# LN1's weight and the q, k, v biases folded into the projection weights; one head of the split tile moved from GpSimd to VectorE

## What is computed

```python
def _ln(x, w, b):
    return (x - m) / jnp.sqrt(v + 1e-05) * w + b
xn = _ln(q_x, ln1_w, ln1_b)                 # q_x is already layer-normed once
q = (xn @ wq + bq); k = (xn @ wk + bk); v = (xn @ wv + bv)      # 16 heads of 16
fq, fk = elu(q) + 1, elu(k) + 1
# per token: mixing over its 16 heads, then a division
qkv = fq @ (fk^T v); qk = fq . sum over heads of fk
x = q_x + (qkv / (qk + 1e-6)) @ wo + bo
x = x + gelu(_ln(x) @ fc_w + fc_b) @ proj_w + proj_b
```

## Time and profile before

| | |
|---|---|
| median of 3 runs | 1744.97 us |
| profiled execution | 1744.85 us, of it a span of 1742.7 us |
| PE busy | 1680.7 us (96%), 7243 instructions |
| PE weight loads | 1227.5 us (70%) |
| VectorE | 1166.9 us (67%) |
| GpSimd | 1166.9 us (67%) |
| ScalarE | 904.1 us (52%) |

### The profile page before, as it was taken

The page is one execution under the profiler, slowest core; times in us unless marked ns, Lnnn a source line. Parts: engine busy times, 40 slices in busy tenths (PEclk is TensorE's granted clock), DMA queues, the critical chain, the costliest instruction groups (busy, mean ns, idle before and its releaser), DMA issues.

```text
span 1742.7 us, 25628 instructions
## 1 busy us (share of the span) xinstructions
PE 1680.7 (96%) x7243; PEld 1227.5 (70%) x7289; DVE 1166.9 (67%) x1968; ACT 904.1 (52%) x2240; POOL 1166.9 (67%) x624
## 2 busy tenths in 40 slices
PE   6899999999999999999999998989999999999997
PEld 4555666666666666666666665578888888888886
DVE  7989999999999999999999993322222222222221
ACT  4356667667667667667667646522322322332322
POOL 5769889889889889889889881413333343343343
PEclk9898999999999999999999999999999999999999
DMA  4302211211211211111111111367777777777764
GB/s 151 116 13 61 62 49 37 62 49 36 61 49 36 61 49 36 59 50 36 54 55 37 37 49 37 92 169 162 165 154 160 165 157 156 167 158 156 168 158 78
DMA packets 89455, 157.20 MB, mean 90 GB/s; under 512 B 8896, under 2 KB 72128, under 8 KB 89024
## 3 DMA queue, kind: packets, MB, share of 16 engines
q1 hardware_dynamic: 60512, 112.58, 20.9%
q0 software_dynamic: 28896, 44.06, 14.9%
HBM read 101.79 MB, written 48.56 MB: 86 GB/s over the span
## 4 chain that ended last, share of the span: by engine, by line
PE 89%; ACT 5%; DVE 2%; issue 2%; DMA 1%; POOL 1%; SPq 1%; POOLq 0%; ACTq 0%; DVEq 0%
PE p_b L1494 17%; PE p_b L1548 13%; PE p_b L1698 10%; PE p_b L1709 10%; PE p_b L1641 8%; PE p_q L1698 7%; PE p_q L1466 6%; PE p_v L1698 4%; PE p_v L1466 3%; PE p_b L1480 2%; PE p_xT L1685 2%; PE p_xT L1626 2%; ACT rows L706 1%; ACT xmid L706 1%; PE p_b L1588 1%
## 5 line engine op out<-in xcount | busy, mean ns | idle before, releaser
L654 POOL DMA_INDIRECT out_rows<-prod_pool,prod x142 | 221.4, 1559 | 387.9 <-ACT prod_pool L949 357.5
L523 POOL TENSOR_TENSOR prod_pool<-prod_pool 128x2048 f32<-128x2048 f32 (+1 forms) x180 | 347.9, 1933 | 14.1
L1548 PE MATMUL p_b<-bT,fc_sb 128*128 128x512 f32 x512 | 231.5, 606 | 1.3 <-ACT bT L865 1.3
L1494 PE MATMUL p_b<-proj_sb,hid 128*128 128x256 f32 x1024 | 230.5, 379 | 0.0
L1494 PEld LDWEIGHTS p_b<-proj_sb,hid 128*128 128x128 f32 x1024 | 189.6, 190 | 29.4 <-issue 0.5
L1026 DVE TENSOR_TENSOR prod<-p_q,eqk 128x4096 f32<-128x4096 f32 (+1 forms) x47 | 184.0, 3914 | 5.3 <-DVE attn L1076 1.0
L1698 PE MATMUL p_b<-prod,exp_up 128*128 128x256 f32 x840 | 187.1, 379 | 0.0
L1063 DVE TENSOR_REDUCE qkv<-prod 128x256 f32<-128x4096 f32 (+1 forms) x47 | 183.7, 3910 | 1.6
L1050 DVE TENSOR_TENSOR prod<-p_q,v_dve 128x2048 f32<-128x2048 f32 (+2 forms) x60 | 177.4, 2956 | 1.5
L574 POOL DMA_INDIRECT rows_sorted<-rows,slot x128 | 125.7, 982 | 78.5 <-issue 34.5
L1035 DVE TENSOR_REDUCE p_q<-prod 128x128 f32<-128x2048 f32 (+2 forms) x60 | 177.4, 2957 | 1.1
(11 more groups left out here) (208 smaller groups left out, 2988.6 us busy)
## 6 DMA issues: line engine op xcount, KB each, us to landing
exp_up<-in_experts SPq DMA_DIRECT2D x71, 768.0 KB
prod<-rows_sorted SPq DMA_DIRECT2D x71, 260.0 KB
xin<-in_x SPq DMA_DIRECT2D x16, 512.0 KB, 3.4
xres<-in_x SPq DMA_DIRECT2D x16, 512.0 KB
xres<-xmid POOLq DMA_DIRECT2D x16, 512.0 KB, 4.6
out_rows<-x SPq DMA_DIRECT2D x16, 512.0 KB, 2.9
exp_dn<-in_experts SPq DMA_DIRECT2D x8, 384.0 KB, 5.8
out_rows<-prod_pool,prod POOLq DMA_INDIRECT x142, 3.8
```

The source lines that it names most:

```text
L523: done(g.tensor_tensor(prod_pool[:, at:at + n * w], prod_pool[:, at:at + n * w], prod_pool[:, at + n * w:at + 2 * n * w], ALU.add))
L654: pool.indirect_dma_start(out=out[:, :], out_offset=bass.IndirectOffsetOnAxis(ap=tok_i[j][:, a:a + 1], axis=0), in_=yg[j][:, a * D:(a + 1) ...
L1494: ins = t_.matmul(o, src[:, k, t * P:(t + 1) * P], w[:, k, :], start=k == 0, stop=bias_at is None and k == chunks - 1)
L1548: ins = t_.matmul(bnk[:], fc_sb[:, k, f * P:(f + 1) * P], bT[:, k, :], start=k == 0, stop=k == KC - 1)
```

## The change

Three things. First, from tile n = 12 on (`FOLDED` = 3 blocks of 4) q, k and v are made from `wfold` instead of `wqkv_sb`: ACT scales the weights by LN1's weight once, PE makes the vector (ln1_b - ln1_w) @ W + bias by two small matmul groups, and VectorE adds a 256th of it to every row of the weights (the diff has two functions `fold()`, VectorE's first and then PE's). `take_x` then adds 1 to the normed x instead of applying weight and bias: the normed x of a token sums to zero over its width, so the ones bring in that vector whole. The bias matmuls are gone for those tiles, and `take_x` is one activation instead of two. Second, this folding is done once, at steps 0 and 1. Third, `POOL_HEADS` is 5, so VectorE has 11 heads of tile 2.

```diff
-POOL_HEADS = 6
+POOL_HEADS = 5
+FOLDED = 3
...
+        def folded(n):
+
+            return not isinstance(n, int) or n >= 4 * FOLDED
...
-                for k in range(KC):
-                    ins = a.activation(xnT[u % 2][:, k, :], p_xT[:, k * P:(k + 1) * P], ACT.Identity,
-                                       bias=ln_sb[:, 1, k:k + 1], scale=ln_sb[:, 0, k:k + 1])
+                if folded(n):
+                    ins = a.activation(xnT[u % 2][:].rearrange("p k t -> p (k t)"), p_xT[:, 0:D], ACT.Identity,
+                                       bias=one_1[:, 0:1])
...
+            def fold_parts():
+
+                for k in range(KC):
+                    a.activation(fold_d[:, k:k + 1], ln_sb[:, 0, k:k + 1], ACT.Identity, scale=-1.0,
+                                 bias=ln_sb[:, 1, k:k + 1]).then_inc(fold_diff, 1)
+                    a.activation(wfold[:, k, :], wqkv_sb[:, k, :], ACT.Copy, scale=ln_sb[:, 0, k:k + 1]
+                                 ).then_inc(fold_in, 1)
+                act.wait_ge(fold_diff, KC)
+                for k in range(KC):
+                    a.activation(fold_w[:, k, :], ident[:], ACT.Identity, scale=0.0, bias=fold_d[:, k:k + 1]
+                                 ).then_inc(fold_in, 1)
...
+                if first:
+                    fold_parts()
                 if more:
                     take_qkv(c + 1, 1)
...
+            def fold():
+
+                dve.wait_ge(fold_psum, 1)
+                dve.wait_ge(fold_in, 2 * KC)
+                for k in range(KC):
+                    for bnk, lo, hi in ((p_b0, 0, 512), (p_b1, 512, 768)):
+                        ins = v.scalar_tensor_tensor(wfold[:, k, lo:hi], bnk[:, 0:hi - lo], 1.0 / D, wfold[:, k, lo:hi],
+                                                     ALU.mult, ALU.add)
...
                     products_2(c, 1, False)
+                if isinstance(c, int) and c == 1:
+                    fold()
...
+                    w = wfold if folded(n) else wqkv_sb
...
-                    if isinstance(n, int) and n == 0:
-                        pe.wait_ge(bias_ready, 1)
-                    for bnk, lo, hi in parts:
-                        ins = t_.matmul(bnk[:, 0:hi - lo], bias_rows_bf[:], bias_bf[:, lo:hi],
-                                        start=False, stop=True)
+                    if not folded(n):
...
+            def fold():
+
+                pe.wait_ge(fold_in, 2 * KC)
+                wait(pe, attnT_ready, KC)
+                for bnk, lo, hi in ((p_b0, 0, 512), (p_b1, 512, 768)):
+                    for k in range(KC):
+                        t_.matmul(bnk[:, 0:hi - lo], fold_w[:, k, :], wqkv_sb[:, k, lo:hi], start=k == 0, stop=False)
+                    ins = t_.matmul(bnk[:, 0:hi - lo], bias_rows_bf[:], bias_bf[:, lo:hi], start=False, stop=True)
...
                     project_x(c, 2, "P")
+                if isinstance(c, int) and c == 1:
+                    fold()
```

More of the change, by code:

```diff
@@ L84, in build @@
         wqkv_sb = sb("wqkv_sb", [P, KC, 3 * D])
+        wfold = sb("wfold", [P, KC, 3 * D])
+        one_1 = sb("one_1", [P, 1])
+        fold_d = sb("fold_d", [P, KC])
         wo_sb = sb("wo_sb", [P, KC, D])
@@ L200, in build @@
         first_s2 = first_s2.rearrange("p (h g) -> p h g", h=HEADS)
+        fold_w = sg_u[:, 1, 0:KC * P].rearrange("p (k n) -> p k n", k=KC)
         first_v = sg_u[:, 0, 0:D].rearrange("p (e g) -> p e g", e=HD)
@@ L257, in build @@
         qkv_taken = sem("qkv_taken")
+        fold_diff = sem("fold_diff")
+        fold_in = sem("fold_in")
+        fold_psum = sem("fold_psum")
+        fold_ready = sem("fold_ready")
         feat_ready = sem("feat_ready")
@@ L674, in take_x @@
                 wait(act, qkv_psum, n - 1)
-                for k in range(KC):
-                    ins = a.activation(xnT[u % 2][:, k, :], p_xT[:, k * P:(k + 1) * P], ACT.Identity,
-                                       bias=ln_sb[:, 1, k:k + 1], scale=ln_sb[:, 0, k:k + 1])
+                if folded(n):
+                    ins = a.activation(xnT[u % 2][:].rearrange("p k t -> p (k t)"), p_xT[:, 0:D], ACT.Identity,
+                                       bias=one_1[:, 0:1])
+                else:
+                    for k in range(KC):
+                        ins = a.activation(xnT[u % 2][:, k, :], p_xT[:, k * P:(k + 1) * P], ACT.Identity,
+                                           bias=ln_sb[:, 1, k:k + 1], scale=ln_sb[:, 0, k:k + 1])
                 ins.then_inc(xnT_ready, 1)
@@ L1136, in first_block @@
                 dve.sem_inc(pq_free, 1)
+            def fold():
[5 more added lines that the diff above has]
+                                                     ALU.mult, ALU.add)
+                        if k < KC - 1 or lo == 0:
+                            done.later(ins)
+                done.sync()
+                announce(dve, ins, fold_ready, 1)
             def residual_1(c):
@@ L1321, in _ @@
             done(v.memset(block_1[:], float(BLOCK)))
+            done(v.memset(one_1[:], 1.0))
             done(v.memset(eps_2[:], EPS * EPS))
@@ L1463, in project_x @@
                     parts = ((p_qk[u % 2], 0, 512), (p_v, 512, 768))
+                    w = wfold if folded(n) else wqkv_sb
                     for bnk, lo, hi in parts:
                         for k in range(KC):
-                            t_.matmul(bnk[:, 0:hi - lo], xnT[u % 2][:, k, :], wqkv_sb[:, k, lo:hi],
-                                      start=k == 0, stop=False)
-                    if isinstance(n, int) and n == 0:
-                        pe.wait_ge(bias_ready, 1)
-                    for bnk, lo, hi in parts:
-                        ins = t_.matmul(bnk[:, 0:hi - lo], bias_rows_bf[:], bias_bf[:, lo:hi],
-                                        start=False, stop=True)
-                    ins.then_inc(qkv_psum, 1)
+                            ins = t_.matmul(bnk[:, 0:hi - lo], xnT[u % 2][:, k, :], w[:, k, lo:hi],
+                                            start=k == 0, stop=folded(n) and k == KC - 1)
+                    if not folded(n):
+                        if isinstance(n, int) and n == 0:
+                            pe.wait_ge(bias_ready, 1)
+                        for bnk, lo, hi in parts:
+                            ins = t_.matmul(bnk[:, 0:hi - lo], bias_rows_bf[:], bias_bf[:, lo:hi],
+                                            start=False, stop=True)
+                    ins.then_inc(qkv_psum, 1)
+            def fold():
+                pe.wait_ge(fold_in, 2 * KC)
+                wait(pe, attnT_ready, KC)
+                for bnk, lo, hi in ((p_b0, 0, 512), (p_b1, 512, 768)):
+                    for k in range(KC):
+                        t_.matmul(bnk[:, 0:hi - lo], fold_w[:, k, :], wqkv_sb[:, k, lo:hi], start=k == 0, stop=False)
+                    ins = t_.matmul(bnk[:, 0:hi - lo], bias_rows_bf[:], bias_bf[:, lo:hi], start=False, stop=True)
+                ins.then_inc(fold_psum, 1)
             def transpose_block(src, banks, ready, tile_ready=None):
@@ L1557, in body @@
                     wait(pe, out_ready, c - 2)
+                    if isinstance(c, int) and c == 1:
+                        pe.wait_ge(fold_ready, 1)
                     if stage_c and more:
```

## The result

| | before | after |
|---|---|---|
| median | 1745.08 us (1744.45 to 1746.4, 4 runs) | 1774.27 us (1764.81 to 1779.6, 4 runs) |
| profiled execution | 1744.85 us, span 1742.7 | 1779.6 us, span 1777.7 |
| twelve steps, from step 3's output projection to step 15's | 790.76 us | 821.99 us |

The changed kernel is slower by a factor of 1.0159 (95% interval 1.0136 to 1.0183). The direction was forecast. The size was not: 29 us instead of 8, and outside the range.

The account below looks back on a forecast made before the run. Bound: the ring through VectorE's last product and PE's tile 1 projection. Twelve steps +7.5, step 2 -0.6, behind step 15 +1.1 sum to +8.0 us on 1744.85, so 1753 us; range 1744 to 1763.

Parts of the forecast that it names:

- The busy line is not the bound; the load that waits 0.12 us behind VectorE's product is.: Tile 1's projection: its first weight load waits for VectorE's last product of tile 3, although PE is 96% busy.
- Bias matmuls out: -0.33 in the ring.: Tile 1's projection: dropping its two bias matmuls shortens the cycle through VectorE and PE by 0.33 us a step.
- the ring: Cycle from VectorE's output-projection step through its last product, PE's tile 1 projection and output projection: 65.74 us before.
- The head: +1.07.: VectorE's tile 2: four long instructions with 256 more elements each add 1.07 us a step, ahead of PE's release.
- New step 66.48, twelve of them +7.5 us.: Steps 3 to 15: each step grows from 65.85 to 66.48 us, together 7.5 us more.
- GpSimd idle 2.5 to 3.3 us.: GpSimd, with one head less, stands idle some 2.5 to 3.3 us before each block's first product.
- `fold` in steps 0 and 1 at nothing.: One-time weight folding on ACT, PE and VectorE fits into existing waits and costs 0 us.
- Step 2 at -0.6.: Step 2: the head meets existing waits and PE comes earlier without biases; -0.3 to -0.6 us, taken as -0.6.
- Behind step 15 at +1.1.: Steps 15 to 16: PE waits for VectorE's attention output, so the head counts whole, +1.1 us.
- A granted clock of 1.00 from step 3 to 15.: PE was to keep its full clock through the twelve steps, despite waiting about 1.95 us in each.
- PE's clock falls in the new wait: Rival, tile 1's projection: each fall costs 1.9 to 3.7 us, total up to 1797; chance 0.08 few, 0.03 many.
- Waits "hardly any elsewhere".: Each step: PE idles 1.8 to 2.0 us ahead of tile 1's projection and hardly anywhere else.

Follow-up runs that it names:

- two kernels with the further sum: Change with six GpSimd heads and GpSimd's gate product moved earlier, plus a VectorE sum ahead of (1772.44 us) or behind (1742.4 us) tile 1's release.
- the head alone: The kernel before with GpSimd's share at five heads and nothing folded: 1763.03 us, ratio 1.0094.
- kernel with filler and early gate: Changed kernel, GpSimd's gate product ahead of three halvings, one group of shared-expert up matmuls computed twice ahead of tile 1's projection: 1754.38 us, ratio 1.007.
- six heads and the early gate: Changed kernel with six heads on GpSimd and its gate product moved ahead of three halvings: 1740.08 us, ratio 0.997.
- six heads and no early gate: Changed kernel with GpSimd keeping six heads of tile 2, its gate product not moved: 1748.21 us, ratio 1.0015.
- the one with the early gate: Changed kernel, five heads on GpSimd, with GpSimd's gate product moved ahead of three halvings: 1772.55 us, ratio 1.0174.

## Why the prediction was right or wrong

- *The busy line is not the bound; the load that waits 0.12 us behind VectorE's product is.* Right. The two kernels with the further sum show it: only what stands ahead of the release lengthens the step by its full time.
- *Bias matmuls out: -0.33 in the ring.* Right: a step without a fall is 66.91 with the head alone and 66.58 with both (from the kernel with filler and early gate; the changed kernel has no such step).
- *The head: +1.07.* Right, a little low: 66.58 against 65.48 with six heads and the early gate is 1.10. The instructions are as forecast, by the groups by form:

```profile
L1057 DVE TENSOR_TENSOR prod<-p_q,eqk 128x2816 f32<-128x2816 f32 x12 | 37.1, 3092 | 1.6
```

  That is 0.267 more than the earlier trace rows have for 2560. The Trainium skill (Perfetto Trace Analysis, Optimizing Scalar/DVE Operations) doubts that moving work between GpSimd and VectorE helps, since they share a read port. No effect of that kind shows in these instructions: VectorE's products of 4096 elements take 4425 ns with five heads on GpSimd as with six, and 4424 to 4426 in the changed kernel whether GpSimd works through 57% or 98% of one.
- *New step 66.48, twelve of them +7.5 us.* The step is 66.58, and the twelve, without falls, take 800.01: +9.25. That is right but for a tenth of a microsecond a step and a little more in two disturbed steps. (12 x 0.63 is 7.6; the sum has 7.5.)
- *GpSimd idle 2.5 to 3.3 us.* About right: 3.1 to 3.6 in all but one of the twelve steps of the kernel with filler and early gate (5.0 in the changed kernel, whose steps are longer).
- *`fold` in steps 0 and 1 at nothing.* Right for PE, whose wait of 5.13 shrinks to 2.23, and for VectorE, whose 2.65 shrinks to 0.61:

```profile
80.66 2.17 PE L1539 MATMUL p_b<-ident,hid 128*128 128x128 f32 x8 [2.23 <-ACT hid L723]
```

```profile
120.45 0.69 DVE L1203 TENSOR_TENSOR x<-xres,p_b 128x512 f32<-128x512 f32 x1 [0.61 <-PE p_b L1556]
```

- *Step 2 at -0.6.* Wrong in sign: the step is 66.96, 0.36 longer than before, not 0.6 shorter. Another 0.51 is there at its start, so that the twelve steps begin 0.87 later than before. Of the 0.51, 0.43 is there already at step 1's output projection, ahead of PE's and VectorE's part of `fold`; the other kernels with the same folding reach that point between 72.89 and 74.32 us, the kernel before at 73.83, so it isn't the folding.
- *Behind step 15 at +1.1.* In the changed kernel it is 2.9 (1777.7 - 1026.98 = 750.72, against 747.82), and 0.4 in the kernel with filler and early gate; neither confirms the 1.1.
- *A granted clock of 1.00 from step 3 to 15.* This is the step that failed. The rival "PE's clock falls in the new wait" was named, with its place and a price a little too high (1.69 us a fall measured, 1.9 to 3.7 forecast), and then given 0.03 for a fall in every step, since 1.95 us is shorter than the 2.48 of the earlier trace rows, behind which the clock had stayed. That one row was taken as a bound, and it is none. In these runs the clock fell behind 1.93 and 2.44 us, and stayed behind 2.11 and 2.78.
- *Waits "hardly any elsewhere".* Wrong too: PE's wait for GpSimd's gate product was overlooked. It has no row before, since there it is 0.44 us of slack; the sum asked what VectorE would wait for, and not what PE, half a microsecond earlier, would meet in the stretch from which the matmuls were taken.

The profiled execution is 35.0 us longer in span. Ahead of the twelve steps 0.87; the ring 9.25 (800.01 - 790.76); falls in the twelve steps 821.99 - 800.01 = 21.98, which is 13 of 1.69; behind them 2.90. This split takes the filler's run for the ring without falls. So 22 of the 35 us are the clock. (The profiled execution is the longest of the four; the median is 5 us shorter.)

What stays open is why, of two waits of like length at one place, one brings a fall and the other doesn't.

## What to carry to other kernels

When a change takes matmuls out of a nearly full TensorE, or makes it wait longer for another engine, list each place where it will now stand still, also those that today are only slack, and price each with a fall of the clock behind it, in every pass of the loop. Work ahead of the instruction that releases another engine and work behind it have different prices, here 31 us (about half of it falls of the clock) and 1 for the same instruction. If the wait must be, a few redundant matmuls in it can be the cheaper way (here 18 us, but only with the other place cured too). Moving a late operand's producer up costs no work at all (here 8 us, with six heads).

## What the hardware showed

- A wait of half a microsecond was enough for a fall (0.49 and 0.51 in the rows at 274.52 and 279.14), where it stood right behind sixteen matmuls of eight columns (1.85 us together); each cost 1.7 us. It was not enough each time: in seven of the twelve steps with six heads and no early gate the clock stayed up behind it, as at 208.75. The Trainium skill (TensorE: Matmul & The Clock Gate, Why this matters for your kernels) warns of idle gaps between bursts of matmuls. The falls at tile 1's projection agree with the warning in kind, but the gaps there (1.93 us at 394.62) are shorter than those it speaks of; at the second place the idle time is a quarter of that. Whether the short matmuls ahead of it count with it wasn't tried.
- A loop can settle into the falls. The steps of the changed kernel and of the one with the early gate became 68.27 us from some step on and stayed within 0.4 of it, one fall in each, at the same place; one step before that took 66.57 in the kernel with the early gate. The executions of the changed kernel spread over 15 us, from 1764.81 to 1779.6. That isn't a mark of falls as such: those of the kernel with the early gate and eleven falls spread over 2.2.
